# A graph-attention kernel on one core: the second epilogue behind group 6, the fourth candidate placement ahead of chunk 30, the last gathered group turn by turn

## What is computed

```
h = relu(layernorm(x));  Wh = h @ W
s = Wh @ a[:128];  d = Wh @ a[128:]
e[i,j] = leaky_relu(s[i] + d[j], 0.2), masked to adj[i,j] > 0 or i == j
x = x + softmax(e, axis=1) @ Wh
weights[i,j] = exp(-(1/adj - 1)**2 / 0.5) if adj[i,j] < 1 else 0
x = x + weights @ (relu(layernorm(x)) @ W1 + B1)
```

## Time and profile before

| | us |
|---|---|
| median of 3 runs (230.5 to 231.35) | 231.09 |
| the profiled execution | 230.85 |
| its span | 229.0 |
| DVE busy (85% of the span) | 195.2 |
| ACT busy (78%) | 178.3 |
| PE busy (67%) | 153.4 |
| POOL busy (55%) | 124.8 |

### The profile page before, as it was taken

The page is one execution under the profiler, slowest core; times in us unless marked ns, Lnnn a source line. Parts: engine busy times, 40 slices in busy tenths (PEclk is TensorE's granted clock), DMA queues, the critical chain, the costliest instruction groups (busy, mean ns, idle before and its releaser), DMA issues.

```text
span 229.0 us, 3107 instructions
## 1 busy us (share of the span) xinstructions
PE 153.4 (67%) x893; PEld 102.3 (45%) x906; DVE 195.2 (85%) x595; ACT 178.3 (78%) x166; POOL 124.8 (55%) x130
## 2 busy tenths in 40 slices
PE   0286789930976956798299865975982697908450
PEld 0285565410455634465166522653750264508340
DVE  7975999908999999997799799689999996998584
ACT  0799983999399999989998879979393989992000
POOL 0198004000001788888759787783588782777600
PEclk9999999995697995999889997799799589785996
DMA  5999999999999999999999999999999994122002
GB/s 158 364 411 410 406 409 409 419 425 406 411 408 407 402 398 391 398 397 401 390 387 399 400 395 397 404 388 399 405 386 400 402 390 181 29 45 98 20 3 97
DMA packets 22388, 76.95 MB, mean 336 GB/s; under 512 B 2643, under 2 KB 3255, under 8 KB 22368
## 3 DMA queue, kind: packets, MB, share of 16 engines
q1 hardware_dynamic: 18624, 70.26, 78.4%
q0 software_dynamic: 3040, 5.34, 6.9%
q10 hardware_dynamic: 704, 1.12, 1.3%
HBM read 74.52 MB, written 4.28 MB: 344 GB/s over the span
## 4 chain that ended last, share of the span: by engine, by line
DMA 30%; DVE 27%; PE 19%; issue 12%; ACT 8%; POOLq 1%; POOL 1%; DVEq 0%; SPq 0%
DMA adj_ring<-in_adj 29%; PE bank L567 9%; DVE summed L1002 6%; ACT spread L814 5%; DVE hub_w L1235 3%; DVE cand L1032 2%; PE bank L669 2%; ACT whe L828 2%; ACT gathered_rows L820 1%; DVE spread L1218 1%; PE bank L554 1%; POOL gathered_rows L470 1%; POOLq L143 1%; DVE stats L979 1%; DMA gathered_rows<-node_table,shared_index 1%
## 5 line engine op out<-in xcount | busy, mean ns | idle before, releaser
L470 POOL DMA_INDIRECT gathered_rows<-node_table,index x48 | 75.4, 1572 | 46.3 <-DVE index L1155 32.9
L845 ACT ACTIVATE trash_a<-adj_ring,below_one 128x4096 fp8e4<-128x4096 f32 x19 | 70.5, 3708 | 11.4 <-DMA adj_ring<-in_adj 10.0
L567 PE MATMUL bank<-adj_ring,pack_w 128*128 128x512 bf16 (+3 forms) x257 | 72.5, 411 | 3.8 <-DMA adj_ring<-in_adj 3.0
L848 ACT ACTIVATE trash_a<-adj_ring 128x4096 fp8e4<-128x4096 f32 x19 | 68.7, 3617 | 0.6
L1002 DVE SCALAR_TENSOR_TENSOR summed<-adj_ring 128x4096 fp8e4<-128x4096 f32 x13 | 57.4, 4419 | 10.2 <-issue 6.6
L567 PEld LDWEIGHTS bank<-adj_ring,pack_w 128*128 128x128 bf16 x262 | 26.8, 106 | 34.9 <-issue 12.0
L470 POOL DMA_INDIRECT gathered_rows<-node_table,shared_index x28 | 34.3, 1225 | 8.5 <-issue 8.2
L669 PE MATMUL bank<-gathered_rows,spread 128*128 128x129 f32 x176 | 24.1, 295 | 7.4 <-DVE spread L1218 4.5
L669 PEld LDWEIGHTS bank<-gathered_rows,spread 128*128 128x128 f32 x176 | 22.7, 208 | 9.0 <-issue 8.9
L1032 DVE MAX8 cand<-bank 128x8 f32<-128x120 f32 (+25 forms) x82 | 23.3, 351 | 0.5 <-PE bank L567 0.5
L554 PE MATMUL bank<-codes,code_w 128*128 128x512 bf16 x24 | 11.0, 459 | 16.8 <-issue 14.9
(11 more groups left out here) (168 smaller groups left out, 228.1 us busy)
## 6 DMA issues: line engine op xcount, KB each, us to landing
adj_ring<-in_adj SPq DMA_DIRECT2D x32, 2048.0 KB, 23.3
node_table<-whe POOLq DMA_DIRECT2D x4, 532.0 KB, 10.9
x_sb<-in_x SPq DMA_DIRECT2D x8, 256.0 KB, 6.4
out<-outb ACTq DMA_DIRECT2D x2, 512.0 KB, 7.5
gathered_rows<-node_table,index POOLq DMA_INDIRECT x48, 5.9
out<-outb SPq DMA_DIRECT2D x1, 512.0 KB, 2.7
gathered_rows<-node_table,shared_index POOLq DMA_INDIRECT x28, 5.4
out<-outb SPq DMA_DIRECT2D x2, 192.0 KB, 2.3
```

What stands on the lines that cost most here:

```text
L470: pool.indirect_dma_start(out=rows[:, g % RING_GROUPS * GE + t, :], out_offset=None, in_=table, in_offset=bass.IndirectOffsetOnAxis(ap=row ...
L567: last = nc.tensor.matmul(to[:, lo:hi], pack_w[:, k, :], ring_hi[:, i % AR, row_at + lo:row_at + hi], start=False, stop=(k == KB - 1), ski ...
L845: nc.scalar.activation(trash_a[:, :], ring[:, i % AR, :], ACT.Sign, bias=below_one[:, :], scale=-1.0, accum_out=signs[:, n:n + 1], saturat ...
L848: nc.scalar.activation(trash_a[:, :], ring[:, i % AR, :], ACT.Abs, accum_out=sizes[:, n:n + 1], saturate=False).then_inc(checked_a, 1)
```

## The change

Four things move or are rewritten:

- The epilogue of row block 1 stands on DVE at i = 28, behind the weighing of group 6, and no longer at i = 27. PE's add_columns of block 2, which waits for it, goes from i = 28 to 29, and the summing of group 6 from 29 to 31. ACT's store of block 1 keeps its place.
- PE's place(3) stands behind add_columns at i = 29, so ahead of chunk 30's packing, and place_shared(3) behind that packing. At the end PE has place(4) ahead of the summing of group 7.
- At the end of DVE's order, decode_shared(3) stands ahead of the last scan, and pick_shared(4) ahead of the third epilogue.
- Group 10 is weighed by turns: each of its four gathers has a semaphore of its own, one TENSOR_SCALAR (multiply, then maximum) takes the place of two products, and PE sums two of the eight outputs per turn. The first of the three final parts stands between the third turn and the fourth.

The diff, without the parts that only declare semaphores or indent:

```diff
@@ -87,6 +87,7 @@
+LAST_TURNS = ROWS_OF_GROUP[-1]
@@ -119,9 +120,12 @@
 ROW_SCORES_AT = {9: [(1, 0), (1, 1)], 18: [(2, 0)], 19: [(2, 1)], 22: [(3, 0)], 23: [(3, 1)]}
 ROW_WEIGHTS_AT = {10: [(1, 0), (1, 1)], 19: [(2, 0)], 20: [(2, 1)], 23: [(3, 0)], 24: [(3, 1)]}
 WEIGH_AT = {13: 0, 15: 1, 18: 2, 21: 3, 24: 4, 25: 5, 28: 6, 31: 7}
-SCATTER_AT = {14: 0, 16: 1, 19: 2, 22: 3, 24: 4, 26: 5, 29: 6}
-ADD_COLUMNS_AT = {13: 0, 21: 1, 28: 2}
-EPILOGUE_AT = {20: 0, 27: 1}
+SCATTER_AT = {14: 0, 16: 1, 19: 2, 22: 3, 24: 4, 26: 5, 31: 6}
+PLACE_AT = {8: 0, 16: 1, 24: 2}
+PLACE_SHARED_AT = {9: 0, 17: 1, 25: 2, 30: 3}
+PLACE_LATE_AT = 29
+ADD_COLUMNS_AT = {13: 0, 21: 1, 29: 2}
+EPILOGUE_AT = {20: 0, 28: 1}
 LATE_CHECK = 25
 STORE_AT = {22: 0, 29: 1}
 
@@ -314,6 +318,8 @@
+        last_gathered = [sem(f"last_gathered{e}") for e in range(LAST_TURNS)]
+        part_weighed, part_masked = sem("part_weighed"), sem("part_masked")
@@ -470,7 +476,8 @@
                     pool.indirect_dma_start(
                         out=rows[:, g % RING_GROUPS * GE + t, :], out_offset=None, in_=table,
                         in_offset=bass.IndirectOffsetOnAxis(ap=row_of.bitcast(u32), axis=0),
-                        bounds_check=N - 1, oob_is_err=False).then_inc(gathered[g % RING_GROUPS], 16)
+                        bounds_check=N - 1, oob_is_err=False).then_inc(
+                            last_gathered[t] if g == GROUPS - 1 else gathered[g % RING_GROUPS], 16)
 
         @block.tensor
         def _(pe):
@@ -683,14 +690,13 @@
                 nc.tensor.matmul(bank[7][0:1, 0:1], whe[:, 0, ONE:ONE + 1], bad[:, :], start=True,
                                  stop=True).then_inc(bad_reduced, 1)
 
-            def scatter_last():
-                g = GROUPS - 1
-                pe.wait_ge(gathered[g % RING_GROUPS], gathered_upto(g))
-                for n, (lo, hi) in enumerate(LAST_PARTS):
-                    pe.wait_ge(part_spread, n + 1)
-                    for t in range(lo, hi):
-                        last = scatter_turn(g, t)
-                    last.then_inc(part_scattered, 1)
+            def scatter_last(e):
+
+                pe.wait_ge(last_gathered[e], 16)
+                pe.wait_ge(part_spread, e + 1)
+                for t in (2 * e, 2 * e + 1):
+                    last = scatter_turn(GROUPS - 1, t)
+                last.then_inc(part_scattered, 1)
 
             def spread_hub():
                 pe.wait_ge(hub_rows_set, 1)
@@ -723,28 +729,31 @@
                     quad_scores(0)
                 if i == PAIR_SCORES_AT:
                     quad_scores(1)
-                if i in PICK_AT:
-                    place(PICK_AT[i])
+                if i in PLACE_AT:
+                    place(PLACE_AT[i])
                 for m in HUB_AT.get(i - 1, ()):
                     hub_group(m)
                 if i == SPREAD_HUB_AT:
                     spread_hub()
                 if i in ADD_COLUMNS_AT:
                     add_columns(ADD_COLUMNS_AT[i])
+                if i == PLACE_LATE_AT:
+                    place(3)
                 if i in SCATTER_AT:
                     scatter(SCATTER_AT[i])
-                if i in DECODE_AT:
-                    place_shared(DECODE_AT[i])
+                if i in PLACE_SHARED_AT:
+                    place_shared(PLACE_SHARED_AT[i])
                 for s, half in ROW_SCORES_AT.get(i, ()):
                     row_scores(s, half)
+            place(4)
             scatter(7)
-            place(4)
             place_shared(4)
             add_columns(SG - 1)
             scatter(8)
             count_bad()
             scatter(9)
-            scatter_last()
+            for e in range(LAST_TURNS):
+                scatter_last(e)
 
             def general_transposes(tr, ev, t):
 
@@ -1209,10 +1218,29 @@
                         quad_of_e[:, :].rearrange("p (o q c) -> p o q c", o=1, c=1).broadcast_to([P, GE * KB, HK, HK]),
                         ALU.mult).then_inc(spread_set, 1)
                 else:
-                    for lo, hi in LAST_PARTS if g == GROUPS - 1 else [(0, KB)]:
-                        for t in range(lo, hi):
-                            last = spread_half(g, t)
-                        last.then_inc(part_spread if g == GROUPS - 1 else spread_set, 1)
+                    for t in range(KB):
+                        last = spread_half(g, t)
+                    last.then_inc(spread_set, 1)
+
+            def weigh_last(e):
+
+                g, n, s = GROUPS - 1, PIECE_OF_GROUP[-1], SG - 1
+                at = g % RING_GROUPS * GE + e
+                weight = shared_w[:, e, :, :].rearrange("p k q -> p (k q)")
+                dve.wait_ge(last_gathered[e], 16)
+                dve.wait_ge(shared_on_set, n + 1)
+                dve.wait_ge(spread_set, g)
+                nc.vector.tensor_scalar(weight, r_pair[:, s // 2, e * KB * HK:(e + 1) * KB * HK],
+                                        rows[:, at, QA:QA + 1], rows[:, at, AA:AA + 1], ALU.mult,
+                                        ALU.max).then_inc(part_weighed, 1)
+                dve.wait_ge(part_weighed, e + 1)
+                nc.vector.tensor_tensor(weight, weight, shared_on[:, n % 2, e, :, :].rearrange("p k q -> p (k q)"),
+                                        ALU.mult).then_inc(part_masked, 1)
+                dve.wait_ge(part_masked, e + 1)
+                dve.wait_ge(scattered, g - 1)
+                for t in (2 * e, 2 * e + 1):
+                    last = spread_half(g, t)
+                last.then_inc(part_spread, 1)
 
             def spread_half(g, t):
                 return nc.vector.tensor_tensor(
@@ -1283,25 +1311,24 @@
-            def last_epilogue():
-                s = SG - 1
-                for n, (lo, hi) in enumerate(LAST_PARTS):
-                    dve.wait_ge(part_scattered, n + 1)
-                    for t in range(lo, hi):
-                        nb = s * KB + t
...
+            def finish_last(n):
+                s, (lo, hi) = SG - 1, LAST_PARTS[n]
+                dve.wait_ge(part_scattered, (hi + 1) // 2)
+                for t in range(lo, hi):
...
@@ -1429,18 +1456,23 @@
                     weigh(WEIGH_AT[i])
                 if i in EPILOGUE_AT:
                     epilogue(EPILOGUE_AT[i])
+            decode_shared(3)
             scan(STEPS - 1)
-            decode_shared(3)
             pick(4)
+            pick_shared(4)
             epilogue(2)
-            pick_shared(4)
             decode_shared(4)
             weigh(8)
             judge()
             weigh(9)
-            weigh(10)
+            weigh_last(0)
+            weigh_last(1)
             set_flag()
-            last_epilogue()
+            weigh_last(2)
+            finish_last(0)
+            weigh_last(3)
+            finish_last(1)
+            finish_last(2)
 
             dve.wait_ge(flag_set, 1)
             general = dve.value_load(flag[0:1, 0:1])
```

23 lines of the change are left out of this document (12 added, 11 removed).

## The result

The changed kernel takes 233.84 us (median of 4 runs, 233.52 to 234.08), the kernel before on the same chip 231.01 us (median of 4, 230.5 to 231.35): a ratio of 1.0123, 95% interval 1.0101 to 1.0146, so 2.8 us slower. The profiled execution took 233.52 us with a span of 231.4 (before: 230.85 and 229.0). Forecast were 234.0 us, a range of 230.4 to 235.2, and slower.

A forecast was written before the change was run, and what follows sets the result against it. The end was taken as bound by POOL's gathers behind the fourth index and DVE's work after the last landing. DVE's end, 229.2 against 226.1, adds 3.1 us to 230.85: 233.95, put as 234.0 us; range 230.4 to 235.2.

The forecast's parts named there:

- The second epilogue: DVE, chunks 27 to 28: moving it uncovers waits of 0.8 and 1.2 us; it ends at 189.9.
- The fourth pick: DVE and PE, step 14: last product at 192.8, index 0.3 us later, last scan at 197.8 to 201.5.
- ACT's queue: ACT's second store waits for the epilogue, checks behind it end at 213.5: 5.8 us less 4.0 slack, 1.8 late.
- the sign: DVE ahead of the verdict: about 2 us of idle would show the prediction right.
- The sum: Program end: group 9 weighed by 218.3, then 3.6, 1.0, 0.1 and 6.2 us: 229.2, 3.1 us later.
- The last group: Group 10 on DVE: 0.92 us a turn, three turns hidden, final series 6.2 us.
- PE's clock: PE at the end: group 9 at 1.2 GHz, the turns after it at 2.4; 1.6 us more.
- (a): Rival at the end: same wait for ACT, but PE at full clock for group 9; 232.4 us, chance 0.22.
- the main case: The end: verdict waits for ACT and PE sums group 9 at the lower clock; 234.0 us, chance 0.45.
- (b): Rival: group 6 lands before 182.2, epilogue ends at 188.8, the waits nearly vanish; 231.2 us, chance 0.15.
- (c): Rival: epilogue ends before 188.2, ACT's slack absorbs the store, POOL's series comes 1.2 us earlier; 229.2 us, chance 0.18.

The follow-up runs named there:

- e4_epilogue_only: The kernel before with only the second epilogue moved behind the weighing of group 6 (column addition and group 6's summing moved along): 233.41 us, ratio 1.0074.
- e7_one_input_check: The changed kernel with chunk 27's check on DVE done as a one-input minimum in place of two inputs: 233.49 us, ratio 1.0093.
- e10_plain_last: The changed kernel with plain transfers of fixed rows in place of the gathers of groups 7 to 9: 234.07 us, ratio 1.0127.
- e6_pe_kept_busy: The changed kernel with unread 128x512 products on PE, 13 ahead of group 8's sum and 11 ahead of group 9's: 234.45 us, ratio 1.0087.
- e0_after_again: The changed kernel itself, run again unaltered on another chip: 236.6 us, ratio 1.0177.

## Why the prediction was right, point by point

**The second epilogue.** Column(27) at 180.17 (180.35 forecast), the weighing at 183.33 (183.4), the epilogue's end at 189.87 (189.9). The two waits of 0.70 and 1.20 us are there as put.

**The fourth pick.** Scan of step 14 at 189.79 (189.95), placed at 192.36 (192.8), the index 0.52 us later than before (0.3). PE had time to place at once and DVE was the late one. The last scan came at 200.59, in the forecast 197.8 to 201.5. The index and the last scan in the kernel before:

```profile
193.31 0.17 DVE L1155 SCALAR_TENSOR_TENSOR index<-words_i,empty_i 128x8 int32<-128x8 int32 x1
...
197.83 1.42 DVE L1032 MAX8 cand<-bank 128x8 f32<-128x272 f32 x4 [0.24 <-PE bank L567]
```

**ACT's queue.** The decisive step. Store at 189.90 (189.9), check at 190.65 (190.7), last end at 213.46 (213.5), verdict at 213.49 (213.6). From issuing the store to the verdict it is 23.59 us in the changed kernel, 23.59 in e4_epilogue_only, 23.59 in e7_one_input_check and 23.59 in e10_plain_last: one queue, wherever the store falls. Group 9's weights were done at 218.21 (218.3). With the epilogue's move alone the time rises by 2.1 of the 2.8 us.

The size of the wait was off: 0.98 us where about 2 was put as the sign. DVE reached the verdict 2.16 us later than before (212.51 against 210.35), since chunk 30 was packed at the lower clock and the last scan came 2.8 us late. The sum allowed for it ("costs nothing" behind a wait of 3.2 us), and so it did. But it means that two paths are late there, and that taking ACT's away alone gives back 0.98 us at most in this execution. In e7_one_input_check and e10_plain_last, on another chip, DVE was ready earlier and the wait was 2.75 and 2.43 us, nearer the forecast.

**The last group.** A turn took 0.97 us (0.30, 0.19 and the two spreads with their gaps) against 0.92 estimated and 0.8 to 1.0 as bounds. The final series ran from 222.88 to 229.11, 6.23 us (6.2). From the verdict to DVE's end it is 15.62 us with the turns (15.77 in e7_one_input_check, 15.32 in e10_plain_last) and 14.92 without (e4_epilogue_only): by these single executions the turns cost 0.4 to 0.85 us, which with the 2.1 of the epilogue comes near the 2.8 us. All four were slow at PE, so this is at like clocks. The placing is left with about nothing.

**PE's clock.** Right in the sum, not in the place. The forecast was group 9 at 3.6 and two turns at full clock, 4.6 us; it was 4.5 (218.36 to 222.88). But it was group 8 that ran wholly at 1.2 GHz (3.65 us), behind an idle stretch of 3.50 us. It began 1.3 us later than forecast (212.66 against 211.4), since DVE weighed it late, so the idle time ahead of group 9 was 1.93 us and not 3.3 to 5.0; group 9 began at full clock, and fell within its own products. That two errors of place gave the right sum is luck. That the lower clock costs time on the path isn't: e6_pe_kept_busy took 1.4 us of it away.

**The rivals.** (a), ACT and full clock, is what e6_pe_kept_busy builds, 1.4 us below the main case (1.6 forecast). (b) and (c) needed an epilogue end at 188.8 or before 188.2; it ended at 189.87. For (c), the index was never early. What (b) hung on, that another execution might not have the long issue, did come up: in e7_one_input_check and e10_plain_last group 6's last issue slipped in ahead of the check. It gained nothing, since DVE was late there itself.

## What to carry to other kernels

Before work is moved on one engine, list the queues that wait for its result in program order: here an untouched engine's store stood ahead of three checks, and 4.0 us of slack met a delay of 5.7. A part that is deferred to let another start earlier also stops covering the waits between them. When an undo experiment misses, look at whether the undone wait is gone in its trace before the theory is dropped, and run the unchanged kernels again beside it, with a profile of each.

## What the runs showed of the hardware

**GpSimd's gather issue is held by a DVE instruction with two SBUF inputs that runs when it begins, and ends 0.87 us behind that.** In the changed kernel the checks of 4.42 us run from 167.96 and 173.58, and issues that begin inside them, at 168.40 and 174.86, end at 173.25 and 178.88: each 0.87 us behind the check's end. The same 0.87 is in e4_epilogue_only (168.87 with 4.84 us against a check that ends at 172.85) and in e7_one_input_check (174.50 against 173.63). Over all profiles here 110 issues begin inside such a check, and each takes 4.0 to 5.2 us and ends 0.86 to 0.88 us behind it. A TENSOR_TENSOR of 1.23 us does the same (the issue at 184.39 takes 1.82 us). Beside the one-input reduction of 4.39 us, two issues that lie wholly within it take 1.00 each. A third, at 178.72, runs past the reduction's end into a TENSOR_SCALAR with one SBUF input (0.80 us from 179.16) and takes 1.35, so two inputs are not the only thing that lengthens an issue. The reduction also writes no 128x4096 output, and no run here parts the two; products that write to SBUF and read one input from PSUM (the epilogue's, before) hold nothing: an issue at 180.64 among them takes 1.00. In e10_plain_last an issue that began 0.03 us ahead of the check took 0.99:

```profile
174.85 0.99 POOL L481 DMA_INDIRECT gathered_rows<-node_table,index  x1 [0.30 <-issue]
```

```profile
174.88 4.43 DVE L1016 SCALAR_TENSOR_TENSOR summed<-adj_ring 128x4096 fp8e4<-128x4096 f32 x1
```

The Trainium skill ("SBUF — State Buffer", "Who interferes with whom") infers of DVE instructions with two SBUF inputs that they do not hold descriptor generation; these gather issues are held, and the measurement decides.

**TensorE's signals came 2 to 10 us behind their rows in the eight profiles of two chips**, while its rows look as always and the granted clock is 1.00 (e0_after_again, 201 to 207 us). The profile shows only a wait of the reader on "remote" or "issue", right behind a product that seems long done. The cause is not known.

**TensorE's clock** fell to 0.50 amid the 28 products after 1.93 us of idle that stood behind 3.65 us of work at 0.50, and stayed at 1.00 where dummy products filled the two idle stretches ahead (e6_pe_kept_busy, 214 to 225 us). The length of the last idle stretch alone does not decide it: in the kernel before it stayed at 1.00 over 3.28 us of idle and the two groups behind that (1.00 in each slice from 213 to 223 us).
